# Spreading the query and key norm factors over the head dimensions by selection matmuls

## What is computed

```
def _rms_norm(t, w):
    return t * jax.lax.rsqrt(jnp.mean(t * t, axis=-1, keepdims=True) + EPS) * w
...
q = (x @ wq.T).reshape(b, s, HEADS, HEAD_DIM)
k = (x @ wk.T).reshape(b, s, HEADS, HEAD_DIM)
v = (x @ wv.T).reshape(b, s, HEADS, HEAD_DIM)
q = _rms_norm(q, q_norm_w)
k = _rms_norm(k, k_norm_w)
q = _apply_rope(q, rope_cos, rope_sin)
k = _apply_rope(k, rope_cos, rope_sin)
q = q / math.sqrt(HEAD_DIM)
```

## Time and profile before

| what | value |
|---|---|
| median of 3 runs | 1897.98 us (1893.78 to 1899.74) |
| profiled execution: span from first to last instruction | 1896.1 us, 1.9 us under the median of the runs |
| PE busy | 1781.2 us (94%) |
| DVE busy | 1620.7 us (85%) |
| ACT busy | 1459.6 us (77%) |
| POOL busy | 344.2 us (18%) |
| query and key stage, first matmul to first matmul of the attention | 311.52 to 386.54 us of the span |

### The profile page before, as it was taken

The page is one execution under the profiler, slowest core; times in us unless marked ns, Lnnn a source line. Parts: engine busy times, 40 slices in busy tenths (PEclk is TensorE's granted clock), DMA queues, the critical chain, the costliest instruction groups (busy, mean ns, idle before and its releaser), DMA issues. The chain is left out here.

```text
span 1896.1 us, 37685 instructions
## 1 busy us (share of the span) xinstructions
PE 1781.2 (94%) x14923; PEld 750.2 (40%) x14923; DVE 1620.7 (85%) x1950; ACT 1459.6 (77%) x2715; POOL 344.2 (18%) x416
## 2 busy tenths in 40 slices
PE   5699998879999999999999999999999999899998
PEld 3488776702222222222222222222222223377786
DVE  6466775689999999999999999999999993386765
ACT  2356564606999999999999999999999996546455
POOL 4266551300000000000000000000000000145565
PEclk9799997857999999999999999999999998999999
DMA  4453330220010010000001001000000010444463
GB/s 117 88 128 127 103 110 1 93 91 2 25 33 20 20 36 22 20 31 27 20 25 33 20 20 37 21 20 31 26 20 26 33 28 3 85 109 109 102 144 78
DMA packets 66309, 98.81 MB, mean 52 GB/s; under 512 B 11995, under 2 KB 33312, under 8 KB 66116
## 3 DMA queue, kind: packets, MB, share of 16 engines
q1 hardware_dynamic: 61974, 94.32, 18.4%
q10 hardware_dynamic: 4160, 2.10, 0.4%
HBM read 84.94 MB, written 11.04 MB: 51 GB/s over the span
## 5 line engine op out<-in xcount | busy, mean ns | idle before, releaser
L1301 DVE TENSOR_REDUCE at_mx<-ps 128x1 f32<-128x1024 f32 x1024 | 1166.1, 1216 | 9.8 <-PE ps L1213 7.7
L1168 ACT ACTIVATE at_prob<-ps 128x512 f32<-128x512 f32 x2048 | 1098.2, 596 | 77.0 <-PE ps L1231 31.8
L1241 PE MATMUL ps<-at_prob,vals 128*32 128x256 f32 x8192 | 656.9, 392 | 13.3 <-ACT at_sums L1175 13.3
L1213 PE MATMUL ps<-k_head,q_head 48*128 48x512 bf16 x2048 | 638.8, 392 | 14.3 <-PEq L800 7.5
L1231 PE MATMUL ps<-q_head,k_head 51*128 51x512 bf16 x1924 | 584.5, 383 | 2.8 <-ACT at_prob L1168 2.8
L1241 PEld LDWEIGHTS ps<-at_prob,vals 128*32 128x32 f32 x8192 | 162.4, 108 | 429.5 <-ACT at_prob L1168 409.0
L688 POOL TENSOR_TENSOR e_part<-e_silu,e_cw 128x512 f32<-128x512 f32 (+1 forms) x208 | 268.1, 1289 | 311.5 <-ACT e_silu L659 124.3
L700 DVE TENSOR_TENSOR ps<-e_part,ps 128x512 f32<-128x512 f32 (+1 forms) x208 | 144.5, 695 | 157.6 <-POOL e_part L688 157.1
L1231 PEld LDWEIGHTS ps<-q_head,k_head 51*128 51x128 bf16 x1924 | 117.5, 93 | 404.1 <-ACT at_prob L1168 385.3
L659 ACT ACTIVATE e_silu<-ps 128x512 f32<-128x512 f32 (+1 forms) x208 | 124.2, 597 | 143.8 <-PE ps L615 141.9
L1095 POOL TENSOR_TENSOR at_mparts<-at_neg,at_zero 128x16 bf16<-128x16 f32 x32 | 7.0, 220 | 796.5 <-DVE at_neg L1315 796.5
(11 more groups left out here) (258 smaller groups left out, 1294.2 us busy)
## 6 DMA issues: line engine op xcount, KB each, us to landing
e_cw<-comb_rows SPq DMA_DIRECT2D x80, 256.0 KB, 3.3
e_cw<-comb_rows SPq DMA_DIRECT2D x32, 224.0 KB, 3.1
e_cw<-comb_rows SPq DMA_DIRECT2D x32, 192.0 KB, 3.3
q_head<-q_rows SPq DMA_DIRECT2D x64, 96.0 KB
k_head<-k_rows SPq DMA_DIRECT2D x64, 96.0 KB
e_cw<-comb_rows SPq DMA_DIRECT2D x32, 160.0 KB, 2.9
e_cw<-comb_rows SPq DMA_DIRECT2D x48, 96.0 KB, 2.8
e_cw<-comb_rows SPq DMA_DIRECT2D x32, 128.0 KB, 3.1
```

Source lines behind the costliest of these rows:

```text
L1168: act.activation(prob[:, g % PROBS, c, :], ps[:, S + bank(i, g, c, last), :], ACT.Exp).then_inc(exped, 1)
L1213: one = pe.matmul(ps[:, at, :], q[i][HALF:HALF + KR, (j // CHUNKS) * P:(j // CHUNKS + 1) * P], k[i][HALF:HALF + KR, c * BLK:(c + 1) * BLK] ...
L1241: done_one = pe.matmul(ps[32 * j:32 * j + 32, O, half * HALF_BLK:(half + 1) * HALF_BLK], vals[i][:, g, :], prob[:, g % PROBS, 2 * half + j ...
L1301: dve.tensor_reduce(mx[i][:, j // 2, j % 2:j % 2 + 1], ps[:, at:at + 2, :].rearrange("p a t -> p (a t)"), AX.X, ALU.max).then_inc(max_redu ...
```

## The change

The reciprocals of a block are not widened. `inv` (128 tokens by 128 factors) is turned once by one PE transpose (`turn_inverses`) into the free half of bank `MEAN`; ACT copies it to a new tile `invT` (factors on partitions, tokens on the free axis); and `spread_back` makes the eight 128x128 pieces by matmuls with a slab of `block_rows` as stationary operand and `invT` as moving one, each row of the result picking the one factor of its head and chunk. For that ACT's root writes its 128 columns in another order (batch index, head, chunk). Both operands are float32, and the products are plain matmuls, not transposes. The semaphore `widened` gives way to `inv_turned` and `inv_kept`.

```
+            def turn_inverses(m):
+                pe.wait_ge(inverted, m + 1)
+                pe.transpose(ps[:, MEAN, FACTORS:FACTORS + P], inv[:], ident[:]).then_inc(inv_turned, 1)
+
             def spread_back(m, i):
-                pe.wait_ge(widened, 2 * m + i + 1)
+                pe.wait_ge(inv_kept, m + 1)
...
                 for j in range(TPB):
-                    last = pe.transpose(ps[:, BACK[i], j * P:(j + 1) * P], rstd[:, m % 2, i, j * P:(j + 1) * P], ident[:])
+                    last = pe.matmul(ps[:, BACK[i], j * P:(j + 1) * P], block_rows[:, i * TPB + j, :], invT[:],
+                                     start=True, stop=True)
                 last.then_inc(spread, 1)
...
                     project(m + 1)
+                turn_inverses(m)
                 spread_back(m, 0)
...
-                act.activation(root[:], ps[:, MEAN, 0:FACTORS], ACT.Sqrt, bias=eps[:]).then_inc(rooted, 1)
+                act.activation(root[:].rearrange("p (i h j) -> p i j h", i=2, j=TPB),
+                               ps[:, MEAN, 0:FACTORS].rearrange("p (i j h) -> p i j h", i=2, j=TPB),
+                               ACT.Sqrt, bias=eps[:]).then_inc(rooted, 1)
                 if m < NB - 1:
                     square(m + 1, 0)
-                act.wait_ge(inverted, m + 1)
-                for i in range(2):
-                    act.activation(rstd[:, m % 2, i, :].rearrange("p (n d) -> p n d", d=HD),
-                                   inv[:, i * TPB * HEADS:(i + 1) * TPB * HEADS].unsqueeze(2).broadcast_to([P, TPB * HEADS, HD]),
-                                   ACT.Copy).then_inc(widened, 1)
+                act.wait_ge(inv_turned, m + 1)
+                act.activation(invT[:], ps[:, MEAN, FACTORS:FACTORS + P], ACT.Copy).then_inc(inv_kept, 1)
...
                 if m >= 1:
-                    dve.wait_ge(widened, 2 * m)
+                    dve.wait_ge(inv_turned, m)
                 dve.reciprocal(inv[:], root[:]).then_inc(inverted, 1)
```

More of the change, by code:

```diff
@@ L151, in build @@
         qk_stored = [sem(f"qk_stored{i}") for i in range(3)]
-        qkv_phase(nc, sem, ps, xnT, (wqT, wkT, wvT), norm_w, head_mean, swap, rope, ident, v,
+        qkv_phase(nc, sem, ps, xnT, (wqT, wkT, wvT), norm_w, head_mean, swap, rope, ident, block_rows, v,
                   q_rows, k_rows, q_head, k_head, qk_loaded, qk_stored)
@@ L759, in _, with qkv_phase @@
                 sp.wait_ge(stored, 16 * NB)
-def qkv_phase(nc, sem, ps, xnT, weights, norm_w, head_mean, swap, rope, ident, v, q_rows, k_rows,
+def qkv_phase(nc, sem, ps, xnT, weights, norm_w, head_mean, swap, rope, ident, block_rows, v, q_rows, k_rows,
               q_head, k_head, qk_loaded, stored):
@@ L775, in qkv_phase @@
     inverted = sem("qk_inverted")
-    widened = sem("qk_widened")
+    inv_turned = sem("qk_inv_turned")
+    inv_kept = sem("qk_inv_kept")
     spread = sem("qk_spread")
@@ L798, in qkv_phase @@
     FACTORS = 2 * TPB * HEADS
+    assert (BATCH, BPS) == (2, TPB) and FACTORS == P
     PARTS = 3
@@ L806, in qkv_phase @@
         inv = tb("inv", [P, FACTORS])
+        invT = tb("invT", [FACTORS, P])
         rstd = tb("rstd", [P, 2, 2, BLK])
```

## The result

The changed kernel is **slower**, by half a per cent: 1904.83 us (median of 4 runs, 1903.82 to 1906.6) against 1896.57 us for the kernel before beside it, a ratio of 1.0047 with a 95% interval of 1.0032 to 1.0062. So the loss is 8 to 13 us where 11.4 was forecast.

What follows compares the result with a forecast made beforehand. The stage's loop was taken to run through PE (root, reciprocal, widening, transposes, values, means). Blocks summed 2 x 1.5 + 1.7 + 4 x 1.3 + 1.5 = 11.4 us, on 1898.0 giving 1909.4 us; range 1902 to 1917.

Steps and rivals of the forecast that it cites:

- Products: Steady block, on PE: 16 float32 instructions at 0.126 us, 2.02 us against 0.91 for the transposes, +1.11.
- Turn, copy and hand-overs: Steady block, from reciprocal to products: PE's transpose, ACT's copy and waits between engines, 0.90 us against 0.72, +0.18.
- The root's other output order: ACT's root in each block: writing its columns in another order costs nothing, bound 0.2 us.
- The Trainium skill's four passes: Products on PE: true float32 takes four passes, 0.213 us a product, 1.71 for eight; a steady block loses 0.31 less.
- ACT's relief: Steady block: ACT has 0.8 us less to do, which gives nothing back because its other work waits for PE and DVE.
- Blocks 0, 1, 2 and 7: Blocks outside the steady ones: 1.5 us lost in each of 0 and 1, 1.7 in 2, 1.5 in 7.
- ACT's: Rival, whole stage: ACT closes the loop, so its lighter work gains 6.3 us, giving 1891.7; chance 0.04.
- the unhidden loads: Rival, products: stationary loads don't hide, 0.21 us an instruction, 10.8 more over eight blocks, 1920; chance 0.04.
- The fall of the clock in a steady block: Rival, blocks 3 to 6: a cold block costs PE 5.7 us more, two of them give 1921; chance 0.06.
- signs of being wrong: Steps of 6.3 us or less, products in 8 instructions, or a granted clock below 1.00 in blocks 3 to 6.
- signs of being right: Blocks 3 to 6: steps of 7.6 us, x16 products about 2 us, PE waiting about 0.8; attention's first matmul near 398.
- The sooner clock: Rival, early blocks: matmuls replacing transposes keep 2.4 GHz, loss 7.4 us, or 5.5 with products at 0.111; chance 0.08.

Runs made afterwards that it cites:

- the second experiment: The changed kernel with ACT's root writing its 128 columns in one run and the means' matmuls writing at a stride of four; 1902.52 us.
- the second execution: The changed kernel run once more with no edit; 1903.55 us, a ratio of 1.0064 to the kernel before.

## Why the prediction was right, and where it was off

The direction and the cause were right: the products are 16 instructions, they stand in PE's part of the loop, and what they take longer than the transposes is the loss. The time, 1904.8, lies in the range (1902 to 1917) and 4.6 under the 1909.4.

Term by term for a steady block. *Products*: forecast 0.126 for an instruction, from the attention's product of the same shape; measured 1.78 / 16 = 0.111, the lower bound, the spacing of the means. Runs with 8, 16 and 32 instructions agree on it. So +0.87 and not +1.11. The Trainium skill's four passes (FP8 and Floating Point Precision, TensorE Precision Notes) gave an estimate of 1.71 for the eight: the trace agrees with it within 0.07. That does not show that passes set the price, since the means, with 16 columns in place of 128, are spaced 0.111 as well. *Turn, copy and hand-overs*: forecast 0.90, measured 0.75, the copy being 0.28 and not the root's 0.36. *The root's other output order*: costed at nothing, with a bound of 0.2; measured 0.12, in every step, and taken away by the second experiment. Together 1.03 to 1.05 and not 1.3. *ACT's relief*: costed at nothing, and the run with the widenings put back shows it; ACT's busy time in a steady step fell by 0.5 us, from 5.19 to 4.68 (the first line of the fence at the end of this section), and not by 0.8.

Blocks 0, 1, 2 and 7 were forecast at 6.2 in sum and came to 4.8 here; the first head's -2.5 has nothing to do with the change. In the second execution, whose head equalled that of the kernel before, the stage lost 83.29 - 75.02 = 8.3, as eight steady blocks at 1.05 would (8.4). The forecast's 11.4 was too much by the price of an instruction (0.24 a block), the turn and copy (0.15 a block) and block 2 (1.7 forecast, -0.6 measured), and too little by the root (0.12 a block) and the fall of the clock in one steady block (1.0). That the sum came nearer than its blocks, which go from -0.6 to +2.1 us by where the clock stood, is luck.

Of the rivals, ACT's fell, and the unhidden loads fell. The fall of the clock in a steady block, given 0.06 with two cold blocks, came in both executions, in one block each, at 1.04 us and not 5.7: PE was cold for part of a block only. A granted clock below 1.00 in blocks 3 to 6 also stood among the prediction's signs of being wrong; it came, for 2.7 us (363.7 to 366.4), while the signs of being right came too: steps of 7.35 where 7.6 was named, and x16 products of 1.8 us; the attention's first matmul stood at 391.48 and 394.00, not near 398. The sooner clock came in block 2, where the step was shorter than before in both executions. The Trainium skill's rule for it (TensorE: Matmul & The Clock Gate, Part 4, PE-mode transpose: the full clock does not come on for transposes) is neither confirmed nor refuted: eight transposes per block, beside other matmuls, went with 1.00 in the kernel before, and eight matmuls of one instruction in the same place mostly with 0.50 in the one profiled execution, but the two kernels differ in the turn and the copy too. The prediction read a swap with gaps around it, and a mean, as what went before the cold stretches of the earlier trace rows. Gaps did not stand before every fall: PE of the changed kernel had no idle time in the 5.40 us before the fall in block 5 (the second line below), and in the order with the values ahead it stayed at half for 35 us without any.

Busy time by stretch in the changed kernel, in the order of the earlier trace rows:

```profile
355.70:363.06 7.36, 6.92 (x52) 6.11 (x52) 4.27 (x7) 4.68 (x10) 2.39 (x2) 1.00 0.33 111
358.00:363.40 5.40, 5.40 (x46) 5.33 (x47) 2.50 (x5) 3.54 (x7) 2.39 (x2) 1.00 0.41 139
```

What brings the clock down in a steady block, and why it does so in one execution and not in another, stays open.

## What to carry to other kernels

Before trading data movement on one engine for arithmetic on another, find which engine the loop waits for: here ACT was relieved of 0.5 us of busy time per block that nobody waited for, and PE, which the loop waited for, got products 0.9 us longer than the transposes. Count what a float32 matmul is in instructions, and price them by a row of the same format from elsewhere in the same program; when two rows differ (0.111 and 0.126), carry both. Look at the clock before believing that shorter work on PE is shorter time.

## What was not expected

- Less work on PE made the kernel slower: eight products of one instruction in place of 16 should have saved 0.9 us per block at full clock, and cost 7 us in the median, with steps of 11.19 us at a granted 0.50 in the profiled execution.
- A PE that never waits can sit at half clock: with the values ahead of the transposes it was busy 35.00 of 35 us at 0.50, in steps of 10.15, against 5.38 in the same execution once the clock was up. What it did there was projection, values, transposes and means back to back. At which clock an execution goes changes from one to the next: 7 of 12 in that order, 5 of 12 with half the projection between transposes and means, and 4 of 60 of the kernel before had a granted clock of 0.956 or less as a mean over the whole. The first two are too close to tell those orders apart, and the cause stays open.
- ACT's root of 128 columns took 0.49 us in place of 0.37 when its output stood four elements apart; PE wrote its results at that stride with the means' 16 instructions at 1.78 us either way.
